# A router's logits summed on VectorE and a projection's bias added on GpSimd, in a kernel that keeps TensorE busy

## The reference

```python
# layer 0: three experts behind a router
nx       = layer_norm(x) * ln_gamma + ln_beta
weights  = softmax(nx @ Wq @ (ctx @ Wk).T / 16)            # 154 per token
combined = concat([nx, weights @ (ctx @ Wv), cond])        # 768 per token
probs    = softmax(combined @ router_W + router_b)         # 3 per token
h        = silu(combined @ e_w1 + e_b1)                    # 3 x 512
routed   = sum_e probs_e * (h_e @ e_w2_e + e_b2_e)
gate     = sigmoid(silu(combined @ gate_w1 + gate_b1) @ gate_w2 + gate_b2)
x        = x + gate * (routed @ out_w + out_b)
# layer 1: attention to the context, 16 heads of 16
xq, xkv  = modulated_layer_norm(x, cond), modulated_layer_norm(ctx, cond)
q, k, v  = xq @ Wq + bq, split(xkv @ Wkv + bkv)
x        = x + (softmax(q k.T / 4) v) @ Wp + bp
```

## Time and profile before

| | us |
|---|---|
| median of 3 runs | 438.75 (437.46 to 439.23) |
| span of the profiled execution | 436.9 |
| TensorE, products | 422.1 busy, 97% of the span, 3629 instructions |
| TensorE, weight loads | 384.7 busy, 88% |
| VectorE | 296.3 busy, 68%, 748 instructions |
| ScalarE | 223.6 busy, 51%, 487 instructions |
| GpSimd | 175.0 busy, 40%, 184 instructions |

### The profile page before, as it was taken

The page is one execution under the profiler, slowest core; times in us unless marked ns, Lnnn a source line. Parts: engine busy times, 40 slices in busy tenths (PEclk is TensorE's granted clock), DMA queues, the critical chain, the costliest instruction groups (busy, mean ns, idle before and its releaser), DMA issues.

```text
span 436.9 us, 9623 instructions
## 1 busy us (share of the span) xinstructions
PE 422.1 (97%) x3629; PEld 384.7 (88%) x3629; DVE 296.3 (68%) x748; ACT 223.6 (51%) x487; POOL 175.0 (40%) x184
## 2 busy tenths in 40 slices
PE   7899999999999999999999999999999899979996
PEld 6578999989998899889998899889988898868876
DVE  2785566674675696739863797389658755891797
ACT  2868643255347543764367246724672356326271
POOL 4545474553353526324523344344433632330020
PEclk9999999999999999999999999999999999998999
DMA  8786102531100210023000300030003021300301
GB/s 288 252 298 269 50 2 47 142 91 31 44 5 1 63 59 30 24 78 116 2 5 13 109 1 5 14 86 0 5 20 80 0 56 28 80 3 26 72 3 48
DMA packets 16837, 27.80 MB, mean 64 GB/s; under 512 B 3800, under 2 KB 9112, under 8 KB 16664
## 3 DMA queue, kind: packets, MB, share of 16 engines
q1 hardware_dynamic: 16664, 27.19, 21.2%
q10 hardware_dynamic: 128, 0.01, 0.0%
HBM read 15.94 MB, written 2.10 MB: 41 GB/s over the span
## 4 chain that ended last, share of the span: by engine, by line
PE 77%; DVE 15%; issue 3%; ACT 3%; DMA 1%; SPq 1%; ACTq 0%
PE hidden_banks L1688 7%; PE hidden_banks L1690 7%; PE hidden_banks L1689 7%; PE score_banks L1695 6%; PE score_banks L2060 5%; PE token_bank L1688 5%; PE token_bank L1689 5%; PE token_bank L1690 5%; PE score_banks L2030 4%; PE value_bank L2083 3%; PE value_bank L2086 3%; PE value_bank L1695 3%; DVE head_maxima L1463 3%; PE hidden_banks L1913 2%; DVE sums L1477 2%
## 5 line engine op out<-in xcount | busy, mean ns | idle before, releaser
L1620 POOL TENSOR_TENSOR hidden_low<-hidden,hidden_high 128x512 fp32r<-128x512 f32 x56 | 72.8, 1300 | 123.5 <-ACT hidden_high L1072 123.4
L1463 DVE TENSOR_REDUCE head_maxima<-score_banks 128x2 f32<-128x308 f32 x128 | 54.6, 473 | 17.1 <-PE score_banks L2030 15.0
L1688 PE MATMUL hidden_banks<-normed_high,hidden_w_high 128*128 128x256 f32 x224 | 64.2, 287 | 0.8 <-issue 0.8
L1689 PE MATMUL hidden_banks<-normed_high,hidden_w_low 128*128 128x256 f32 x224 | 62.5, 279 | 0.0
L1690 PE MATMUL hidden_banks<-normed_low,hidden_w_high 128*128 128x256 f32 x224 | 62.5, 279 | 0.0
L1132 ACT ACTIVATE exp_ring<-score_banks 128x512 f32<-128x512 f32 x96 | 52.6, 600 | 18.8 <-PE score_banks L2060 17.5
L1072 ACT CAST hidden_high<-hidden 128x512 fp32r<-128x512 f32 x56 | 34.8, 622 | 48.2 <-DVE hidden L1380 48.1
L1688 PE MATMUL token_bank<-expert_out_high,hidden_high 128*128 128x256 f32 x192 | 55.7, 290 | 0.0
L1064 ACT ACTIVATE hidden<-hidden_banks 128x512 f32<-128x512 f32 x56 | 33.3, 595 | 41.6 <-PE hidden_banks L1913 40.0
L1690 PE MATMUL token_bank<-expert_out_low,hidden_high 128*128 128x256 f32 x192 | 53.4, 278 | 0.0
L1689 PE MATMUL token_bank<-expert_out_high,hidden_low 128*128 128x256 f32 x192 | 53.4, 278 | 0.0
(11 more groups left out here) (294 smaller groups left out, 1111.5 us busy)
## 6 DMA issues: line engine op xcount, KB each, us to landing
unit_weights<-units SPq DMA_DIRECT2D x7, 768.0 KB, 6.0
query_stack<-queries_high SPq DMA_DIRECT2D x56, 64.0 KB, 2.0
tokens<-x SPq DMA_DIRECT2D x8, 256.0 KB, 3.7
query_stack<-queries_low SPq DMA_DIRECT2D x28, 64.0 KB, 2.0
w_slice<-units SPq DMA_DIRECT2D x7, 256.0 KB, 3.0
out<-tokens SPq DMA_DIRECT2D x7, 256.0 KB, 2.4
w_T<-folds SPq DMA_DIRECT2D x6, 256.0 KB, 6.1
pair_keys<-keys_high SPq DMA_DIRECT2D x16, 77.0 KB
```

What stands on the lines that cost most here:

```text
L1463: v.tensor_reduce(MX[:, s, first:first + step + 1:step], S[:, ring_of[key][0], 0:2 * CTX].rearrange("p (j n) -> p j n", j=2), AX.X, ALU.ma ...
L1620: nc.gpsimd.tensor_tensor(SL[:, ring(t, u), :], TB[:, ring(t, u), :], raw(SH[:, ring(t, u), :]), ALU.subtract).then_inc(gpsimd_h, 1)
L1688: mm(out_, lh, rh, start=start, stop=False, skip_group_check=skip)
L1689: mm(out_, ll, rh, start=False, stop=False, skip_group_check=skip)
```

## The change

Context's share of the logits. The setup no longer makes `router_context`. TensorE instead writes, in six products for batch 0 in the setup ("fold", `router_rows`) and in six for batch 1 in the loop of tile 3 ("rows"), the product of V and router_W with all 128 partitions alike: 3 experts x 154 contexts. VectorE copies it from PSUM into `router_rows` (`VR`), for batch 0 in the setup and for batch 1 ahead of the sums of tile 4. The step "logit" of TensorE is gone. VectorE's step multiplies `PB` by `VR`, for each half and expert, and sums the 154 products into `LG`: six instructions that write their products into `router_terms`, which shares its memory with `XH0`. It no longer waits for TensorE, but for GpSimd's "prob" and "low"; GpSimd's "norm" of the next tile waits for it, as it writes `XH0`. The maximum, the exponential and the normalisation stay. The entry of the step in `PLAN` goes from 14.4 to 12.8 (tile 7: 14.9 to 13.2; tile 1 had 15.4 and has 12.8).

The projection's bias. The two products (2097) are gone. bp is loaded by SyncE in the setup, behind the loads of the tokens, as 128 equal rows (`BP`, 128 KB), and GpSimd adds it to X[t] once ScalarE has read the tokens for layer 1's `x_hat`. VectorE's subtraction of the projection waits for that.

Memory moves with it: layer 1's `x_hat` (`XH1`) now lies where `query_in_low` does and waits for the query products of the tile before; the sums of the attention lie where `XH1` was.

```diff
-    "ln": 0.2, "norm": 1.6, ..., "route": 12.3, "logit": 14.4, "res": 17.4,
+    "ln": 0.2, "norm": 1.6, ..., "route": 12.3, "rows": 13.4, "logit": 12.8, "res": 17.4,
-    "out": (38.34, 56.69), "outl": (43.37, 97.85), "proj": 43.6, ...
+    "out": (38.34, 56.69), "outl": (43.37, 97.85), "bias": 26.2, "proj": 43.6, ...
@@ PLAN_OF
-    1: { "logit": 15.4, "z": 0.62 }        7: { ..., "logit": 14.9 }
+    1: { "z": 0.62 }                       7: { ..., "logit": 13.2, "bias": 21 }
@@ SETUP
-    "sel": 114.7, "unstack": 105, "bias2": (26.4, 26.7), "zero": 102.7,
+    "sel": 114.7, "unstack": 105, "bias2": (26.4, 26.7), "zero": 103.2,
@@ schedule
+        place(at + plan(t, "bias"), ("bias", t))
+    place(FIRST + LOOP * AGAIN + PLAN["rows"], ("rows", 0))
@@ SBUF
+        TERMS = put("router_terms", [P, NSUB, EXPERTS, CTX], offset=xhat_at)
+        XH1 = put("x_hat1", [P, NSUB, D], offset=R1 + 2 * 4 * KC * TILE)
+        VR = put("router_rows", [P, EXPERTS, CTX])
@@ SyncE, setup
+                sp.wait_ge(gpsimd_keyn, upto(gpsimd_keyn, ("keyn", 1), "xh"))
+                sp.dma_start(BP[:, :], a["proj_b"].partition_broadcast(P)).then_inc(proj_b_loaded, 16)
@@ ScalarE, x_hat(t) of layer 1
+                if t:
+                    act.wait_ge(tensor_query, upto(tensor_query, ("query", t - 1), "q"))
@@ VectorE, logit(t)
-                dve.wait_ge(tensor_logit, upto(tensor_logit, key, "l"))
+                dve.wait_ge(gpsimd_prob, upto(gpsimd_prob, ("prob", t), "p"))
                 dve.wait_ge(vector_att, upto(vector_att, ("att", t), "t"))
-                v.tensor_tensor(LG[:, :, :], LG[:, :, :], parts_of[:, 1, :, 0:EXPERTS], ALU.add)...
-                v.tensor_tensor(LG[:, :, :], LG[:, :, :], parts_of[:, 0, :, 0:EXPERTS], ALU.add)...
+                dve.wait_ge(gpsimd_low, upto(gpsimd_low, ("low", t), "n"))
+                ...
+                elif t == TPB:
+                    dve.wait_ge(tensor_rows, upto(tensor_rows, ("rows", 0), "r"))
+                    v.tensor_copy(VR[:, :, :], H[:, 0:EXPERTS * CTX].rearrange("p (e n) -> p e n", e=EXPERTS)).then_inc(
+                        vector_results, results.one())
+                    dve.wait_ge(vector_results, results.n)
+                for s in range(NSUB):
+                    for e in range(EXPERTS):
+                        last = v.tensor_tensor_reduce(out=TERMS[:, s, e, :], in0=PB[:, s, 0:CTX], in1=VR[:, e, :], scale=1.0,
+                                                      scalar=LG[:, s, e:e + 1], op0=ALU.mult, op1=ALU.add,
+                                                      accum_out=LG[:, s, e:e + 1])
+                last.then_inc(vector_logit, 1)
@@ VectorE, proj(t) and last_add
+                dve.wait_ge(gpsimd_bias, upto(gpsimd_bias, key, "x"))
@@ GpSimd, norm(t)
+                    pool.wait_ge(vector_logit, upto(vector_logit, ("logit", t - 1), "l"))
@@ GpSimd, new step "bias"
+            def projection_bias(key):
+                t = key[1]
+                pool.wait_ge(scalar_xhat, upto(scalar_xhat, ("xhat", t), "xh"))
+                ...
+                x = X[:, t % SLOTS, :, :]
+                nc.gpsimd.tensor_tensor(x, x, BP[:, :].unsqueeze(1).to_broadcast([P, NSUB, D]), ALU.add).then_inc(gpsimd_bias, 1)
@@ TensorE, fold(b): the small products of V and router_W
+                if b == 0:
+                    router_rows(S[:, 0, :], b)
@@ TensorE, new
+            def router_rows(bank, b):
+                for e in range(EXPERTS):
+                    last = plain(bank[:, CTX * e:CTX * e + CTX],
+                                 [(RW[:, KC + k, e:e + 1].to_broadcast([P, P]), VL[b][:, k, 0:CTX]) for k in range(KC)])
+                return last
+            def rows_again(key):
+                pe.wait_ge(vector_route, upto(vector_route, ("route", TPB), "dl"))
+                router_rows(H[:, :], 1).then_inc(tensor_rows, 1)
@@ TensorE, norm(t)
-                    pe.wait_ge(vector_logit, upto(vector_logit, ("logit", t - 1), "l"))
+                    pe.wait_ge(vector_route, upto(vector_route, ("route", t - 1), "dl"))
+                    if t == TPB + 1:
+                        pe.wait_ge(vector_logit, upto(vector_logit, ("logit", TPB), "l"))
@@ TensorE, logit(t): six products, removed
-                    mm(H[:, 8 * s:8 * s + 8], PTh[:, t % 2, c], VRC[:, b, 0, :], ...)
-                    mm(H[:, 8 * s:8 * s + 4], PTl[:, t % 2, c], VRC[:, b, 0, 0:4], ...)
-                    last = mm(H[:, 8 * s:8 * s + 4], PTD[0:STACK, t % 2, c], VRC[0:STACK, b, 1, 0:4], ...)
@@ TensorE, proj_part
-                    if g == 0:
-                        mm(proj_bank(t, s), BSEL[:, 1 + EXPERTS:2 + EXPERTS].to_broadcast([P, P]), CB[:, :], start=False, stop=False)
```

More of the change, by code:

```diff
@@ L153 @@
         "prob": ["p"],
-        "logit": ["l"],
+        "rows": ["r"],
         "z": ["z"],
@@ L281 @@
     "dup": (37.2, 49.2), "za": -0.4, "step": 1.99, "z": 0.38, "h": 1.5, "p": 3.3, "again": -6.4, "vw": -38.8,
-    "ln": 0.2, "norm": 1.6, "low": 6.6, "att": 7.9, "prob": 9.1, "route": 12.3, "logit": 14.4, "res": 17.4,
+    "ln": 0.2, "norm": 1.6, "low": 6.6, "att": 7.9, "prob": 9.1, "route": 12.3, "rows": 13.4, "logit": 12.8, "res": 17.4,
     "qn": 18.4, "shift": 18.5, "xhat": 19.3, "qx": 19.54, "qlow": 20.1, "query": 20.7,
@@ L287 @@
     "value": (33.88, 34.18, 35.92, 36.25), "raw": (35.5, 36.9), "sum": (35.3, 36.4), "sums": (38.1, 47.7),
-    "out": (38.34, 56.69), "outl": (43.37, 97.85), "proj": 43.6, "last": (16, 59.3), "reload": 45.3, "init": 5.2,
+    "out": (38.34, 56.69), "outl": (43.37, 97.85), "bias": 26.2, "proj": 43.6, "last": (16, 59.3), "reload": 45.3, "init": 5.2,
 }
@@ L296 @@
     1: {
-        "logit": 15.4, "z": 0.62,
+        "z": 0.62,
     },
@@ L310 @@
     7: {
-        "route": 13.2, "most": (19.2, 19.2, 19.3, 19.4, 19.4, 19.6, 20.3, 20.5), "init": 5.6, "sums": (28.4, 36),
+        "route": 13.2, "most": (19.2, 19.2, 19.3, 19.4, 19.4, 19.6, 20.3, 20.5), "init": 5.6, "sums": (28.4, 36), "bias": 21,
         "za": -0.73, "score": (22.06, 22.59, 22.73, 23.07, 23.16, 23.16, 23.63, 23.73, 24.03, 24.23, 24.34, 24.54),
         "outl": (33.4, 33.8), "row": (19.96, 21.53), "h": 1.2, "p": 3.5, "last": (39.5, 39.7), "query": 18.06,
-        "xhat": 17.7, "ln": 0.5, "value": (23.2, 23.5, 24.7, 25.8), "proj": 38, "logit": 14.9, "out": (27.3, 33.2),
+        "xhat": 17.7, "ln": 0.5, "value": (23.2, 23.5, 24.7, 25.8), "proj": 38, "logit": 13.2, "out": (27.3, 33.2),
         "raw": (23.1, 28.7), "qlow": 18, "qx": 17.62, "dup": (24.9, 28.7), "step": 1.96,
@@ L548, in build @@
         WS = put("w_slice", [P, 2, KC, UCOLS])
-        VTT1 = put("values_T1", [P, KC, P])
-        LT = [put(f"tail_rows{b}", [P, KC, 32]) for b in range(BATCH)]
-        SCW2, KTT, VTT0, OB, used0 = run(keys_at, [
+        VL1 = put("values_T1", [P, KC, P + 32])
+        SCW2, KTT, VL0, OB, used0 = run(keys_at, [
             ("query_score_w_raw", [P, KC, D], F32), ("keys_T", [P, KC, 160], F32),
-            ("values_T0", [P, KC, P], F32),
+            ("values_T0", [P, KC, P + 32], F32),
             ("out_b_row", [P, D], F32)])
@@ L563, in build @@
         SCW = [part[:, KC * 160:].rearrange("p (k n) -> p k n", k=KC) for part in (FW0, FW1)] + [SCW2]
-        VTT = (VTT0, VTT1)
+        VL = (VL0, VL1)
+        VTT = [part[:, :, 0:P] for part in VL]
+        LT = [part[:, :, P:P + 32] for part in VL]
+        at[0] += 256
         hidden_at = at[0]
@@ L637, in build @@
         WQR = put("query_w_raw", [P, KC, D])
[L638 removed]
+        SUM, BP, NMH, NML, _ = run(setup_at, [("sums", [P, TILE], F32), ("proj_bias", [P, D], F32), ("max_high", [HEADS, TILE], F32R),
                                           ("max_low", [HEADS, TILE], F32R)])
@@ L1675, in _ @@
             parts = {"setup2": setup_values, "gsplit": gate_split, "unit": unit, "split": split, "keyn": keyn, "ln": ln, "norm": norm, "prob": prob,
-                     "low": low, "h": hidden, "qn": qn, "zero": zeros, "sel": select, "sum": sums}
+                     "low": low, "h": hidden, "qn": qn, "zero": zeros, "sel": select, "bias": projection_bias, "sum": sums}
             for key in order("gpsimd"):
@@ L1891, in prob @@
                 last.then_inc(tensor_prob, 1)
-            def logit(key):
-                t = key[1]
-                b = t // TPB
-                pe.wait_ge(vector_route, upto(vector_route, ("route", t), "dl"))
-                for s in range(NSUB):
-                    c = slice(P * s, P * s + P)
-                    mm(H[:, 8 * s:8 * s + 8], PTh[:, t % 2, c], VRC[:, b, 0, :], start=(s == 0), stop=False, skip_group_check=True)
-                    mm(H[:, 8 * s:8 * s + 4], PTl[:, t % 2, c], VRC[:, b, 0, 0:4], start=False, stop=False, skip_group_check=True)
-                    last = mm(H[:, 8 * s:8 * s + 4], PTD[0:STACK, t % 2, c], VRC[0:STACK, b, 1, 0:4], start=False, stop=True,
-                              skip_group_check=True)
-                last.then_inc(tensor_logit, 1)
```

(2 more changed lines are left out.)

60 lines of the change are left out of this document (27 added, 33 removed).

## The result

The changed kernel takes 462.37 us (458.96 to 464.24, four runs), the kernel before 438.2 us (437.46 to 439.23) beside it: a ratio of 1.053, interval 1.050 to 1.057. The profiled execution has a span of 462.2 us, 25.3 more than before, with a mean granted clock of 0.974 (before 0.996). Ratios and their intervals leave out runs that took over 1.5% more than the fastest of the same kernel: here only split_late has such runs, two of its four, the profiled one among them.

What follows compares the result with a forecast made beforehand. TensorE and, from 299 to 305 us, VectorE were taken to be at their limit. Span 436.9 + 21.65 (stretches) + 2.5 (hold) = 461.1 us, the median 1.85 us above the span, so 463 us; range 440 to 476.

Steps and rivals of the forecast that it cites:

- The place decided: VectorE's step moves ahead of the last maxima and work that TensorE and GpSimd await: 463 us; forecast's chance 0.66.
- tiles 5 and 6: Step ahead of maxima and statistics delays GpSimd's chain and the gate products by D - 0.55, 3.3 us each, 6.6 us.
- tiles 0 and 1: x_hat waits for the six sums and hidden stands behind the step: 2.0 us each, 4.0 us.
- tiles 2 to 4: Last two maxima fall behind the step, row step waits 3.25 us a loop; with tile 4's row copy 9.85 us.
- tile 7: VectorE's outs_low falls behind the step and delays the projection that reads it: 1.2 us.
- D: Length of VectorE's logit step with six sums of 0.39 us: 3.84 us (3.27 to 4.45), against 1.8 before.
- The hold: A VectorE sum held until GpSimd's hidden_low ends, in tiles 5 and 6: 2 x 1.25 = 2.5 us (0 to 2.5).
- The rows of the second batch: Setup products counted zero within 1 us; VectorE's copy from PSUM in tile 4 0.6 us; TensorE's loop products unpriced.
- The clock: Rival: the clock falls in all seven loops from tile 1 on, adding up to 12 us, 475 us; chance 0.14.
- TensorE alone decides: Rival: VectorE's step fits its 32% idle time and TensorE's 6.6 us are kept: 432.2 us, faster; chance 0.13.
- The bias: GpSimd's bias pass, 1.29 us per tile, lies in a gap between two hidden_low: counted zero.

Runs made afterwards that it cites:

- split_late: Changed kernel with VectorE's step at entry 18.0, its products where x_hat lies, and the normalisation a step of its own: 455.39 us, ratio 1.030.
- back_own: Changed kernel with VectorE's step back at 14.4 (tile 1 15.4), its products written where the normed tokens lie, freeing x_hat: 445.88 us, ratio 1.015.
- clock_kept2: Changed kernel with 28 useless products, into a free bank, ahead of TensorE's row step in the first five tiles: 457.05 us, ratio 1.042.
- back_tile1: back_own with the step of tile 1 alone at entry 13.4 instead of 15.4: 444.23 us, ratio 1.011.
- bias_only: Kernel before with the projection's bias alone moved to GpSimd, the logits as they were: 438.37 us, ratio 0.998.

## Why the prediction was right

The place decided, as forecast: 463 us predicted, 462.4 measured, the row step waiting in five loops (2.6 to 3.9 us, 3 to 3.25 forecast), x_hat and the gate late in tiles 5 and 6, VectorE's sums ahead of the maxima, PE's share at 92%. That the sum came out within 1 us is luck, since terms off on either side cancelled. By stretches, forecast and measured growth are 4.0 and 2.8 us in tiles 0 and 1, 9.85 and 15.3 in tiles 2 to 4, 9.1 and 7.8 in tiles 5 and 6, 1.2 and 0.7 in tile 7, and 0 and -1.3 behind it.

- **D**, the length of a step, was 3.84 us; it measured 3.28 (in tile 0 from the first sum at 32.85 to the next step's start at 36.13 us), 0.56 us less, and 4.29 where the hold is in it (322.25 to 326.54 above). The row that I took, ScalarE's accumulator read with 0.10 us from start to start, was the wrong neighbour: VectorE's read is there (0.08 us) but the next sum starts at the same moment, 0.30 us after the last, as in the earlier trace rows. The Trainium skill ("VectorE: DVE Perf Modes", "Two Vector instructions with no wait between them") is right that such an operation is two instructions; the trace shows that the second cost nothing here.
- **The hold** beside hidden_low: 1.25 us in each of tiles 5 and 6 predicted, 1.03 us measured (a sum of 1.40 us at 322.54 and at 274.70, 0.37 as a rule). It ends 0.2 us behind GpSimd's hidden_low (322.29 + 1.47). In back_own, where the step stands beside hidden_low in tile 1, it is 1.42 us too. The Trainium skill ("SBUF — State Buffer", "SBUF: two separate sides") calls the shared ports a lock for a whole instruction; the trace agrees, and shows one sum of the six held, since GpSimd's operation was then over.
- **Tiles 2 to 4** without the clock: 9.85 us predicted; with the clock kept, clock_kept2's stretches to the gates of tiles 2, 3 and 4 grew by 3.2, 2.5 and 4.0 us, 9.6 in all. Tile 4's has the term that I left out, the rows.
- **Tiles 5 and 6**: the number was near, the path was not the one that I priced. I counted D - 0.55 us through the statistics and GpSimd's chain to the gate products. In the profile after, TensorE's long wait in each of the two stretches is the one of 3.90 us for the maxima, and the chain is over 0.8 us before the gate. The slow clock behind the wait is part of that: in clock_kept2 the two stretches grew by 2.6 and 3.7 us, and in tile 6 hidden_low ends at 326.25, 0.1 us before the gate products at 326.35. The two paths are nearly as long, so naming the wrong one cost the sum little.
- **The rows of the second batch.** I counted the setup's products at zero within 1 us, which holds: the rows of the first batch hold TensorE for 1.57 us (10.84 to 12.41), and the short products that went, of both batches, had held it for 0.68 and 0.67 us (10.67 to 11.35 and 55.93 to 56.60 in the kernel before). To the rows in tile 3's loop I gave no price at all, and they hold TensorE for 226.30 - 224.83 = 1.47 us. Net that is 1.7 us of TensorE, against 0.58 us saved a tile. TensorE's timeline:

```profile
224.83 1.74 PE L1724 MATMUL head_bank<-values_T,constants 128*128 128x154 f32 x12
...
226.30 0.39 PE L1717 MATMUL hidden_banks<-normed_high,hidden_w_high 128*128 128x256 f32 x1
```

- **Tiles 0 and 1**: 4.0 us predicted, 2.8 measured, nearly all of it in the first stretch. There the reason that I gave is seen: tile 1's x_hat waits for the six sums of tile 0 and starts at 34.94 instead of 32.29 us, and TensorE waits for it:

```profile
37.43 0.66 PE L1909 MATMUL head_bank<-constants,x_hat 128*128 128x128 f32 x4 [1.19 <-POOL x_hat L1651]
```

- **The clock** stood as a rival, with 0.14 and 12 us on top; it came true in five loops, for 5 to 8 us, which the sum does not hold. My reason against it (in tiles 5 and 6 the slow products lie inside a wait) held in part: the stretches to the gates of tiles 4 to 6 are 0.7 to 0.8 us shorter with the clock kept, those to tiles 2 and 3 are 2.4 and 2.6 us shorter.
- **TensorE alone decides** was wrong as a rival, and it did not win in the other orders that were tried either: the best, back_tile1, is still slower than before, and the rows take back a net 1.7 of the 4.6 us that the six products save in eight tiles.
- **The bias** at zero or a little gain was right.

Open: which of the remaining 6 us of back_tile1 against bias_only (7.4 by the spans) are the setup (its first two stretches are 3.7 us longer than bias_only's, rows included), and which VectorE's length in later loops. It was not taken apart further.

## What to carry to other kernels

Before work is moved to an engine with idle time, look at the stretch in which it will stand, not at the share of the span, and count who waits behind it. A scratch buffer shared with the next stage's input can leave a step without a good place: price the buffer with the order. And a saving that recurs has to carry the one-off work that makes it possible, here a net 1.7 us for 0.58 us a tile.

## What the runs showed of the hardware

A wait of TensorE can be paid twice: after a stretch in which TensorE was busy 0.51 of 4 us the granted clock was 0.50 for the next five, and with the waits filled it was 1.00 and the kernel 5 to 8 us shorter. A step 0.9 us shorter in five loops gave 10.8 us, not 4.5, with the clock falling behind two of the waits instead of five. Behind a sum of products on VectorE over 154 columns, written out beside its accumulator, the next one starts after 0.30 us, as behind an operation with two inputs alone. One such sum took 1.40 us instead of 0.37 where a GpSimd operation of 1.47 us had begun beside it.
